# A Mamba block and two local-attention layers on one core: enter's silus together, the clipping of the norms on POOL, a feed-forward over three banks, and new orders of issue

## The reference

```python
x = x + LN(mamba(LN(x)))        # mamba: u, z = x @ in_proj; u = silu(conv4(u)); dt = softplus(...)
                                # state = exp(dt*a)*state + dt*b*u over 512 steps, 256 channels x 16 states
                                # y = (sum over states of state*c + D*u) * silu(z); out_proj
x = x + LN(layers(LN(x)))       # two layers, each:
#   h = shift(x); q, k, v = h @ wqkv (8 heads of 64)
#   q, k = q/max(|q|, 1e-12)*scale, k/max(|k|, 1e-12)*scale; rotary; attention in windows of 64
#   x = x + o @ wo
#   h = LN(shift(x))*g + b; a, g = split(h @ w1 + b1) (341 each); x = x + (a*gelu(g)) @ w2 + b2
```

## Time and profile before

| | |
|---|---|
| median of 3 runs | 2785.74 us (2784.07 to 2799.39) |
| the profiled execution's own time | 2779.99 us |
| its span | 2778.2 us |
| busy in the span | PE 81%, DVE 72%, ACT 70%, POOL 63% |
| granted TensorE clock, mean | 0.921 |
| table loads on ACT | 173, of 1283 ns each |

### The profile page before, as it was taken

How to read it: one execution, slowest core, us unless ns; L and a number is a source line. 1 busy time by engine, 2 the same in 40 slices (tenths; PEclk the granted TensorE clock), 3 DMA queues, 4 the chain that set the end, 5 groups by cost and what they waited for, 6 DMA issues and landing times. The chain is left out here.

```text
span 2778.2 us, 44164 instructions
## 1 busy us (share of the span) xinstructions
PE 2252.5 (81%) x15936; PEld 1256.8 (45%) x15936; DVE 2008.3 (72%) x3735; ACT 1945.3 (70%) x4142; POOL 1759.0 (63%) x1540
## 2 busy tenths in 40 slices
PE   2257788897979898797979888897989889797967
PEld 0014354453636454453636445463635445363635
DVE  1557686878778686978778686877878687877442
ACT  2255768787877878787777868787777878766543
POOL 0868585867758585866757586766858585773010
PEclk8577899999999999999999999899989999999976
DMA  2543323324233323324332322424332322420000
GB/s 108 140 115 93 94 64 108 77 71 115 75 107 88 93 76 96 92 69 111 81 107 81 100 69 81 107 66 115 88 104 72 106 73 76 107 73 12 5 4 8
DMA packets 107146, 231.26 MB, mean 83 GB/s; under 512 B 7728, under 2 KB 48688, under 8 KB 106672
## 3 DMA queue, kind: packets, MB, share of 16 engines
q1 hardware_dynamic: 106928, 228.44, 30.2%
HBM read 185.42 MB, written 42.99 MB: 82 GB/s over the span
## 5 line engine op out<-in xcount | busy, mean ns | idle before, releaser
L645 POOL TENSOR_TENSOR gy<-hs,bc 128x512 f32<-128x512 f32 x512 | 650.2, 1270 | 354.6 <-DVE hs L600 204.0
L600 DVE TENSOR_TENSOR_SCAN hs<-da,dbu 128x512 f32<-128x512 f32 x512 | 623.3, 1217 | 173.1 <-issue 71.9
L628 POOL TENSOR_TENSOR dbu<-spread,bc 128x512 f32<-128x512 f32 x512 | 650.6, 1271 | 38.6 <-DMA spread<-steps 38.6
L576 ACT ACTIVATE da<-spread,rest 128x512 f32<-128x512 f32 x512 | 354.1, 692 | 176.5 <-DVE hs L600 163.7
L553 PE MATMUL y_sum<-gy,rest 128*32 128x512 f32 x1024 | 289.6, 647 | 94.8 <-POOL gy L645 94.8
L671 PE MATMUL b_bank<-rest,h_t 128*128 128x512 f32 x384 | 230.2, 715 | 86.9 <-DVE qr L848 83.8
L671 PE MATMUL f_bank<-rest,h_t 128*128 128x512 f32 x384 | 232.2, 715 | 54.4 <-ACT h_t L740 29.4
L86 ACT ACT_TABLE_LOAD x173 | 222.0, 1283 | 51.5 <-PE f_bank L926 21.9
L826 DVE TENSOR_REDUCE ss<-sq 128x8 f32<-128x512 f32 x256 | 173.0, 676 | 116.6 <-ACT sq L750 116.0
L806 ACT ACTIVATE late<-b_bank,mx 128x128 f32<-128x128 f32 x512 | 145.9, 368 | 111.8 <-DVE mx L868 111.8
L897 POOL TENSOR_TENSOR qr<-qr,rn 128x512 f32<-128x512 f32 x128 | 132.6, 1042 | 137.1 <-ACT rn L774 136.8
(11 more groups left out here) (181 smaller groups left out, 5277.5 us busy)
## 6 DMA issues: line engine op xcount, KB each, us to landing
spread<-steps SPq DMA_DIRECT2D x256, 512.0 KB, 4.6
steps<-k_t SPq DMA_DIRECT2D x32, 512.0 KB, 2.8
bc<-bc_rows SPq DMA_DIRECT2D x32, 512.0 KB, 8.5
gate<-gates SPq DMA_DIRECT2D x32, 512.0 KB, 5.6
gates<-kr SPq DMA_DIRECT2D x16, 512.0 KB, 3.1
gates<-late SPq DMA_DIRECT2D x16, 512.0 KB, 3.6
sq<-in_x SPq DMA_DIRECT2D x16, 256.0 KB, 2.9
x<-in_x SPq DMA_DIRECT2D x16, 256.0 KB, 3.8
```

Of the source, the lines that this page charges most:

```text
L576: e.activation(da[:, :], spread[:, slot(b, s // 2), 0, :], ACT.Exp, scale=a_neg[:, s:s + 1]).then_inc(decayed.sem, 1)
L600: e.tensor_tensor_scan(hs[:, s % 2, :], da[:, :], dbu[:, s % 2, :], 0.0, ALU.mult, ALU.add).then_inc(scanned.sem, 1)
L628: e.tensor_tensor(dbu[:, s % 2, :], spread[:, slot(b, s // 2), 1, :], bc[:, s % 2, :], ALU.mult).then_inc(fed.sem, 1)
L645: e.tensor_tensor(gy[:, s % 4, :], hs[:, s % 2, :], bc[:, 2 + s % 2, :], ALU.mult).then_inc(read_out.sem, 1)
```

## The change

1. Enter: the third tap is written to `u` (SBUF, tile `late`) and no longer to the bank; both silus run there in place, one after the other, after both taps. PE's projections now wait for the convolution and not for the silu.
2. The eight Relus a round on ACT are gone. POOL takes the maximum with 1e-24 in place (`TENSOR_SCALAR`, 128x16) as steps of its own, and ACT's Ln waits for it.
3. `f0`, the front's feed-forward, uses three banks and three gelu buffers: g0, g1, a0, g2, a1, a2 in banks L1, L2, L0, L1, L0, L2. `f1` keeps its two banks.
4. All five `ORDER` strings are new.

```diff
@@ ORDER (one line of it)
-    "sp": "M15 E1 M5 S1 M2 S1 B1 S3 B1",
+    "sp": "M17 E1 M2 B1 M2 S1 M1 S1 B1 S3",
@@ FeedForward
-                self.L0, self.L1 = w.banks[0:2]
+                L0, L1, L2 = self.L0, self.L1, self.L2 = w.banks
+                if w is wf:
+                    self.parts = [("g0", L1, None), ("g1", L2, None), ("a0", L0, None), ("g2", L1, "gelu0"),
+                                  ("a1", L0, "gate0"), ("a2", L2, "gelu1")]
+                else:
+                    self.parts = [("g0", L1, None), ("a0", L0, None), ("g1", L1, "gelu0"), ("a1", L0, "gate0"),
+                                  ("g2", L1, "gelu1"), ("a2", L0, "gate1")]
@@ dve_enter
-                    e.scalar_tensor_tensor(e_bank[:, :], x_pad[:, h, k:k + T], conv_w[:, h, k:k + 1], e_bank[:, :],
+                    into = u[:, h, :] if k == NCONV - 2 else e_bank[:, :]
+                    e.scalar_tensor_tensor(into, x_pad[:, h, k:k + T], conv_w[:, h, k:k + 1], e_bank[:, :],
@@ pe_enter
-            for i, before in enumerate((e_copied(b), u_made(b, 0), u_made(b, 1), z_made(b, 0))):
+            for i, before in enumerate((e_copied(b), conv_step(b, 2), conv_step(b, 5), z_made(b, 0))):
@@ act_enter
                 yield
+            for h in range(NH2):
                 E.wait_ge(*conv_step(b, 3 * h + 2))
                 E.use_table(SILU)
-                e.activation(u[:, h, :], e_bank[:, :], ACT.Silu).then_inc(u_made.sem, 1)
+                e.activation(u[:, h, :], u[:, h, :], ACT.Silu).then_inc(u_made.sem, 1)
@@ act_attention, inverse_norms
-                E.wait_ge(*w.summed(b, 2 * g + 1))
-                e.activation(part(w.lg), part(w.ss), ACT.Relu, bias=minus_tiny).then_inc(w.clipped.sem, 1)
-                yield
                 E.wait_ge(*w.clipped(b, g))
                 E.use_table(EXP_LN)
-                e.activation(part(w.lg), part(w.lg), ACT.Ln, bias=tiny).then_inc(w.logged.sem, 1)
+                e.activation(part(w.lg), part(w.ss), ACT.Ln).then_inc(w.logged.sem, 1)
@@ pool_attention
+            def clip(g):
+                E.wait_ge(*w.summed(b, 2 * g + 1))
+                e.tensor_scalar(w.ss[:, 2 * g:2 * g + 2, :], w.ss[:, 2 * g:2 * g + 2, :], TINY, None, ALU.max).then_inc(
+                    w.clipped.sem, 1)
...
-            for take in "q0 q1 v0 k0 v1 k1 q2 q3 v2 v3 k2 k3".split():
+            for take in "c0 q0 q1 v0 c1 k0 v1 k1 c2 q2 q3 v2 v3 c3 k2 k3".split():
@@ act_feed_forward
-                if c == 2:
+                if c == 2 and f is f1:
                     E.wait_ge(*f.gated(b, 0))
```

More of the change, by code:

```diff
@@ L43 @@
     "pe": (
[3 rows of a table removed]
[3 rows of a table added]
     "act": (
[4 rows of a table removed]
[4 rows of a table added]
     "dve": (
[6 rows of a table removed]
[4 rows of a table added]
+    "pool": (
+        "A3 M2 A1 B1 M2 A1 M1 B1 A1 B2 M2 B1 M2 B1 M1 B1 A1 B1 M2 B1 A1 M2 B1 A1 M1 B2 M1 A2 B2 A1 B2 A1 M1 A1 M2 "
+        "A2 M47 B1 M1 E4"),
+    "sp": "M17 E1 M2 B1 M2 S1 M1 S1 B1 S3",
 }
@@ L134, in build @@
         maskb = sb("maskb", [P, NT * P], BF16)
-        columns = sb("columns", [P, 4])
-        eps, tiny, minus_tiny, log8 = (columns[:, n:n + 1] for n in range(4))
+        columns = sb("columns", [P, 2])
+        eps, log8 = (columns[:, n:n + 1] for n in range(2))
         tab = sb("tab", [P, DEPTH, 4, NT, DH])
@@ L205, in __init__ @@
                 self.after, self.norm = w, Norm(f"_ff{n}")
-                self.L0, self.L1 = w.banks[0:2]
+                L0, L1, L2 = self.L0, self.L1, self.L2 = w.banks
[5 more added lines that the diff above has]
+                                  ("g2", L1, "gelu1"), ("a2", L0, "gate1")]
+                self.bank = {part: bank for part, bank, _ in self.parts}
                 self.h = w.sq[:, 0, :].rearrange("p (t d) -> p t d", t=NT)
-                self.h_t, self.ge = w.qr[:, 0, :], w.kr[:, 0:2, :]
+                self.h_t, self.ge = w.qr[:, 0, :], w.kr[:, 0:3 if w is wf else 2, :]
                 self.ff = w.vs[:, 1:, :, :].rearrange("p t h d -> p (t h d)")[:, 0:3 * T].rearrange("p (c n) -> p c n", c=3)
@@ L903, in pair @@
                 e.tensor_copy(w.vs[0:WIN, t, :, :], w.v[0:WIN, t, :, :]).then_inc(w.v_paired.sem, 1)
-            for take in "q0 q1 v0 k0 v1 k1 q2 q3 v2 v3 k2 k3".split():
-                (pair(int(take[1])) if take[0] == "v" else normalise(take))
+            for take in "c0 q0 q1 v0 c1 k0 v1 k1 c2 q2 q3 v2 v3 c3 k2 k3".split():
+                if take[0] == "c":
+                    clip(int(take[1]))
+                elif take[0] == "v":
+                    pair(int(take[1]))
+                else:
+                    normalise(take)
                 yield
@@ L922, in pe_feed_forward @@
             E.wait_ge(*f.copied(b))
[L923 to L930, removed]
-                else:
-                    E.wait_ge(*f.right(b))
-                e.matmul(L0[0:n, :], w1[:, l, c0:c0 + n], f.h_t, start=True, stop=True).then_inc(f.a_projected.sem, 1)
+            E.wait_ge(*f.right(b))
+            for part, bank, after in f.parts:
+                c = int(part[1])
+                c0, n = HCH[c]
+                if after:
+                    E.wait_ge(*(f.gelu_made if after[:-1] == "gelu" else f.gated)(b, int(after[-1])))
+                if part[0] == "g":
+                    e.matmul(bank[0:n, :], w1[:, l, HID + c0:HID + c0 + n], f.h_t, start=True,
+                             stop=True).then_inc(f.g_projected.sem, 1)
+                else:
+                    e.matmul(bank[0:n, :], w1[:, l, c0:c0 + n], f.h_t, start=True, stop=True).then_inc(f.a_projected.sem, 1)
                 yield
@@ L964, in act_feed_forward @@
                 E.wait_ge(*f.g_projected(b, c))
-                if c == 2:
+                if c == 2 and f is f1:
                     E.wait_ge(*f.gated(b, 0))
                 E.use_table(GELU)
-                e.activation(f.ge[0:n, c % 2, :], L1[0:n, :], ACT.Gelu,
+                e.activation(f.ge[0:n, c if f is f0 else c % 2, :], f.bank[f"g{c}"][0:n, :], ACT.Gelu,
                              bias=b1[0:n, l, 3 + c:4 + c]).then_inc(f.gelu_made.sem, 1)
@@ L982, in dve_feed_forward @@
                     E.wait_ge(*f.ones_set(b))
-                e.scalar_tensor_tensor(f.ff[0:n, c, :], L0[0:n, :], b1[0:n, l, c:c + 1], f.ge[0:n, c % 2, :], ALU.add,
-                                       ALU.mult).then_inc(f.gated.sem, 1)
+                e.scalar_tensor_tensor(f.ff[0:n, c, :], f.bank[f"a{c}"][0:n, :], b1[0:n, l, c:c + 1],
+                                       f.ge[0:n, c if f is f0 else c % 2, :], ALU.add, ALU.mult).then_inc(f.gated.sem, 1)
                 yield
@@ L1067, in dve_constants @@
         def dve_constants(E, e):
-            for column, value in ((eps, EPS), (tiny, TINY), (minus_tiny, -TINY), (log8, math.log(8.0))):
+            for column, value in ((eps, EPS), (log8, math.log(8.0))):
                 e.memset(column, value)
```

## The result

| | before | after |
|---|---|---|
| median | 2784.9 us (2781.86 to 2799.39) | 2716.81 us (2709.4 to 2723.21, 4 runs) |
| the profiled execution's own time and span | 2779.99, 2778.2 us | 2723.21, 2721.4 us |
| granted clock, mean | 0.921 | 0.948 |

A forecast was written before the change was run, and what follows sets the result against it. No single engine bounds throughout: DVE, PE, then ACT bound a round's three stretches. Terms -2.1 - 0.5 + 0.6 = -2.0 us a round, twelve rounds -24, drain -9, together -33: 2747, forecast as 2753 us; range 2705 to 2798.

The forecast's parts named there:

- ACT's idle time in the third stretch: From the first copies of front's attention output to the next front's two copies: 0.3 us more waiting for statistics and x_proj.
- The sum of moved work: ACT between front's first output copies and the next front's copies: -3.85 - 1.38 + 1.64 + 1.91 = -1.7 us a round.
- the earlier copy: Behind the state's norm, the next front's copy waits only for PE's turn of x, starting 0.7 us sooner.
- Front's scores earlier, -0.5: Between back's first scores and front's first output copies: front's scores follow two heads of back instead of three, -0.5 us.
- One scan more, +0.6: DVE ahead of back's first scores: one more scan of 1217 ns, half to two thirds absorbed, +0.6 us, bounds 0 and +1.2.
- The drain, -9: Behind the last enter, where front and back run with little else: 7 table loads fewer, counted whole, -9 us.
- Relus, 0: 128 Relus leave ACT, 2.4 us a round, nearly all before back's first scores; hidden by DVE's chain, 0.
- Clips at 0.3 us, 0 on the path: POOL's maximum steps: 0.3 us each, eight a round, 2.4 us on POOL before back's first scores, 0 on the path.
- The +2.6 us between the two pairs of copies: Between the copy pairs of front's output: 1.9 us of enter's work and one 0.69 us gelu added, already in the sum.
- All of ACT's saving on the path: Rival: ACT's whole saving, 61.6 + 38.2 = 100 us, shortens the kernel, giving 2686 us; chance 0.17.
- Given back: Rival: PE's products and y sums delay front's output product, returning 2 to 3 us a round; 2777 to 2789 us, chance 0.24.
- POOL as the bound: Rival: before back's first scores, clips and stalled scan feeds make POOL the bound; +35 us, 2821 us, chance 0.14.

The follow-up runs named there:

- The lone silu: The changed kernel with the first silu put back on its own ahead of the second pad and tap, 155 loads: 2765.35 us.

## Why the prediction was wrong in size and right in sign

**The failed step is ACT's idle time in the third stretch.** The prediction forecast 0.3 us more of it, walking the new order by hand, and said of the three banks that their gain "is not a term of its own". The stretch was to lose 2.1 us and lost 3.5. Split at the end of the state's norm (1103.39 before), the terms compare like this, as medians of twelve rounds:

| ACT, third stretch | before | after | change | forecast |
|---|---|---|---|---|
| busy up to the end of the state's norm | 37.26 | 35.57 | -1.7 | -1.7 |
| idle up to there | 3.89 | 2.73 | -1.2 | +0.3 |
| from there to the end of the front's two copies | 2.62 | 1.99 | -0.6 | -0.7 |

The sum of moved work is right, the last norm's +1.64 included, as that scaling did move from behind the state's norm to ahead of it; so is the earlier copy. What was wrong is the waits. The rows are ACT alone up to the state's norm, before and after:

```profile
1062.25:1103.39 41.14, 37.25 (x59) 1.00 0.20 60
```

```profile
1199.16:1237.47 38.31, 35.57 (x61) 1.00 0.17 51
```

The longest of the waits in them, before and after:

```profile
ACT L86 <- PE f_bank L926: 1.4, 2, 0.9
ACT qr L960 <- PE f_bank L331: 0.8, 1, 0.8
ACT kr L968 <- PE f_bank L926: 0.6, 1, 0.6
```

```profile
ACT lv_ff L321 <- DVE mv_ff L314: 0.7, 1, 0.7
ACT xs L336 <- DVE mr_x L330: 0.5, 1, 0.5
ACT kr L988 <- PE f_bank L950: 0.4, 1, 0.4
```

Before, ACT waited 2.0 us for the front's g and 0.8 for the turn ahead of its scale; 0.4 of these 2.8 us is left. The new waits that the prediction named, for the front's statistics and x_proj, came (0.7 and 0.3 us) and are smaller. With -1.2 in place of +0.3 the sum for the stretch is -3.5, as measured. The run with two banks is the test: it gives back 2.0 us of waiting for g and, in all, 3.2 us of the stretch. The three banks alone, on the old order, took 1.1 us off those waits, and the wait for the state's statistics came in their place.

**Front's scores earlier, -0.5:** mis-sized, -1.2. The front's first scores now come 4.2 us earlier behind the back's, while the way from there to P1 grew by 3.0 only. The wait that the prediction took as its reserve, for ACT's exponentials, hardly fell (1.4 to 1.2 us, 0.8 and 0.4 in two rows), so where the gain comes from stays open.

**One scan more, +0.6:** measured +0.6.

**The round:** -3.9 by medians instead of -2.0, and thirteen rounds instead of twelve. Their 54 us are nearly the whole difference of the traces, 56.8.

**The drain, -9:** mis-sized, -3.8. The seven loads were counted from the start of the last enter (27 and 20), and three of them still stand in the thirteenth round. Behind its end the traces have 16 loads before and 12 after: four, 5.1 us, of which 3.8 came through. No run was made on that part.

**Relus, 0:** right; putting them back costs 1 us, which is within the noise. **Clips at 0.3 us, 0 on the path:** right in this order; one takes 0.244 us. On the old orders they cost 63 us, by ACT's Ln waiting for them and DVE's sums for the squares behind it, a path that the prediction did not name.

**The gelus:** side by side, and the third starts 2.4 us behind the first, where "within 3" was said. Without the three banks 48 us are lost. The lone silu is worth as much again, 49. These don't add up to the gain: each undone part meets orders that were made for it.

**The +2.6 us between the two pairs of copies:** from start to start 3.73 to 5.97, so +2.2, and the residual came later as said. From it to the first gelu the way became 0.7 us shorter.

**Rivals.** All of ACT's saving on the path, 2686, is refuted: 3.85 us a round in the second stretch and the Relus are worth nothing. What was right in it is that ACT counts in two stretches, not in one. The prediction said that the first is hidden by DVE's chain; one load there costs 16 us. DVE is full there, but its sums need ACT's squares, and a load ahead of the wrong square delays the whole chain. That error hurt no term, since no load was removed there and the Relus were worth nothing. Given back, 2777 to 2789: refuted, as the second stretch became shorter. POOL as the bound, by clips that stall the scan's feeds: not in either order. The scans' waits for `dbu` are 52 us before, 51 with the clips alone on the old orders and 46 after the change.

**The drain of a table switch** of the Trainium skill ("ScalarE: Activation LUTs", What ACT_TABLE_LOAD costs) was set aside, and the runs agree. In the timeline above the instruction ahead of the load ends at 1226.94, the load starts at 1226.96, and the gelu follows at 1228.25, 1.29 us later. Where 48 loads were added and nothing else was changed, they cost at most 47 us, 0.98 us each, under their own 1.283 and far from 2.66. The 30 loads of the split silus cost 1.6 us each, but there the silu moved too and DVE's queue waited for it.

**Open** are where the second stretch's 1.2 us come from, the last 1.3 us of the drain, and how far the clock takes part. It was 0.90 to 0.97 in the first stretch of the changed kernel and 0.85 to 0.97 with three loads in the third.

## What to carry to other kernels

A sum of moved work is only half of a forecast: here it was right to a tenth of a microsecond, and the waits between the work made the miss. List the waits that the trace shows in the stretch, and where a change removes the reason for one (a third bank, for the waits for g), give that wait a term of its own. In a kernel whose queues follow a written order, judge an edit of code together with that order: here the same three edits are worth +118 us without it and -68 with it. To price work on an engine, add the same few microseconds to one stretch at a time; the answers lay between 0 and 47 us.

## What the hardware did that I had not expected

The granted clock fell in single rounds of one kernel and made them longer. With the same instructions the second stretch took 62.6 us at 1.00 and 68.1 at 0.90. Two such rounds came in the kernel with three loads behind the front's norms. In the profiled executions of before and after the clock in that stretch was 1.00 in all twelve steady rounds.

The front's projections of q, k and v, on PE in the first stretch, took 715 ns each before and 667 after:

```profile
L671 PE MATMUL f_bank<-rest,h_t 128*128 128x512 f32 x384 | 232.2, 715 | 54.4 <-ACT h_t L740 29.4 <-DVE qr L848 24.7
```

```profile
L683 PE MATMUL f_bank<-rest,h_t 128*128 128x512 f32 x384 | 215.3, 667 | 32.0 <-ACT h_t L752 20.5 <-DVE qr L857 11.5
```

The mean clock of the first stretch was 0.88 before and 0.93 after. The clock shows in the way from the front's copies to its first sum, which PE's first projections set. One such window of before and one of after, PE alone:

```profile
1106.01:1108.80 2.79, 2.74 (x4) 0.50 0.60 220
```

```profile
1239.45:1241.30 1.85, 1.79 (x4) 1.00 0.57 208
```

At the upper level (1.00, 2.4 GHz) it takes 1.85 us, at the lower (0.50, 1.2 GHz) 2.79. After the change both occur: six of twelve rounds are at 1.00 there, and two at 0.50 with 2.79 us again. So of the 2.4 us by which DVE's wait for the first squares is shorter in the two rounds shown above (6.05 and 3.69), 0.9 is the clock. Over twelve rounds this evens out (means of 2.32 before and 2.27 after), and the rest of the first stretch does not follow the clock: before, it took 48.2 us at 0.95, 0.91 and 0.85 alike.

A small activation has its price in its operands too. The Ln of 128x16 took 309 ns with its bias column (before) and takes 211 without it (after):

```profile
L767 ACT ACTIVATE lg<-lg,columns 128x16 f32<-128x16 f32 x128 | 39.5, 309 | 3.2
```
